# Turning the next expert's five row tiles in three groups of one, two and two

## What is computed

```python
capacity = max(1, math.ceil(N / E * CAPACITY_FACTOR))          # 4096 / 8 * 1.25 = 640 rows per expert
... # each token goes to its two best experts, as far as these have room
h = gelu(einsum('ecd,edh->ech', buf, w1) + b1[:, None, :])     # 640 x 256 by 256 x 1024
out = einsum('ech,ehd->ecd', h, w2) + b2[:, None, :]           # 640 x 1024 by 1024 x 256
y = einsum('ned,ne->nd', gathered, weights)                    # sum over a token's experts, by gate
x = layernorm(x + y)
```

## Time and profile before

| | |
|---|---|
| median of 3 runs | 917.41 us (916.76 to 917.43) |
| profiled execution, its own time | 918.83 us |
| its span in the trace | 917.0 us |
| mean granted TensorE clock | 0.986 of 2.4 GHz |
| TensorE busy | 878.5 us, 96% of the span |
| ScalarE busy | 736.7 us, 80% |
| VectorE busy | 635.7 us, 69% |
| GpSimd busy | 481.5 us, 53% |

### The profile page before, as it was taken

How to read it: one execution, slowest core, us unless ns; L and a number is a source line. 1 busy time by engine, 2 the same in 40 slices (tenths; PEclk the granted TensorE clock), 3 DMA queues, 4 the chain that set the end, 5 groups by cost and what they waited for, 6 DMA issues and landing times. The chain is left out here.

```text
span 917.0 us, 20105 instructions
## 1 busy us (share of the span) xinstructions
PE 878.5 (96%) x7673; PEld 498.4 (54%) x7673; DVE 635.7 (69%) x1177; ACT 736.7 (80%) x911; POOL 481.5 (53%) x408
## 2 busy tenths in 40 slices
PE   7999999999999999999999999999399999999995
PEld 5434344433344434334443433333299999999995
DVE  5788556547886645799565577527657887888786
ACT  5698978897897899889789889898355787778875
POOL 3388245245575635657563454441512556666574
PEclk9999999999999999999999999999789999999998
DMA  5644456643535345263433525612170745534411
GB/s 176 161 131 140 145 211 222 226 168 106 185 128 213 119 131 208 87 206 135 165 110 111 195 87 182 205 54 84 60 244 32 242 151 185 172 115 134 157 63 64
DMA packets 62508, 135.47 MB, mean 148 GB/s; under 512 B 10558, under 2 KB 31398, under 8 KB 62272
## 3 DMA queue, kind: packets, MB, share of 16 engines
q1 hardware_dynamic: 41648, 72.61, 24.4%
q0 software_dynamic: 20464, 61.18, 19.0%
q10 hardware_dynamic: 288, 0.27, 0.1%
HBM read 69.20 MB, written 62.35 MB: 143 GB/s over the span
## 5 line engine op out<-in xcount | busy, mean ns | idle before, releaser
L814 ACT ACTIVATE prob<-spsum 128x1024 f32<-128x1024 f32 x512 | 492.7, 1022 | 83.0 <-PE spsum L1036 79.2
L1060 PE MATMUL opsum<-prob,val 128*17 128x512 f32 x2048 | 270.1, 597 | 3.9 <-ACT prob L814 1.9
L1036 PE MATMUL spsum<-stacks 32*128 32x512 f32 x1536 | 135.5, 426 | 2.0 <-issue 1.3
L1036 PEld LDWEIGHTS spsum<-stacks 32*128 32x128 f32 x1536 | 73.5, 183 | 117.0 <-ACT prob L814 65.8
L1036 PEld LDWEIGHTS spsum<-area_q 32*128 32x128 f32 x1536 | 73.1, 183 | 112.7 <-ACT prob L814 57.1
L1036 PE MATMUL spsum<-area_q 32*128 32x512 f32 x1536 | 132.7, 425 | 1.1 <-ACT prob L814 1.1
L1452 DVE RECIPROCAL oden<-oden 128x256 f32<-128x256 f32 x62 | 108.7, 1753 | 2.1
L608 POOL TENSOR_TENSOR area_s<-emb,area_s 128x1024 fp32r<-128x1024 f32 x28 | 66.7, 2380 | 48.4 <-DVE area_s L1259 45.0
L694 POOL TENSOR_TENSOR onorm<-oraw,oden 128x512 f32<-128x512 f32 x31 | 42.1, 1358 | 93.3 <-DVE oden L1452 93.2
L1060 PEld LDWEIGHTS opsum<-prob,val 128*17 128x17 f32 x2048 | 39.4, 95 | 84.9 <-ACT prob L814 46.2
L606 POOL TENSOR_TENSOR square<-raw 128x512 bf16<-128x512 f32 x28 | 52.5, 1877 | 56.4 <-DVE raw L1232 56.3
(11 more groups left out here) (278 smaller groups left out, 1375.8 us busy)
## 6 DMA issues: line engine op xcount, KB each, us to landing
split_scratch<-area_s POOLq DMA_DIRECT2D x56, 512.0 KB
area_k<-in_w SPq DMA_DIRECT2D x16, 1024.0 KB, 6.9
area_q<-split_scratch SPq DMA_DIRECT2D x28, 512.0 KB
stacks<-split_scratch SPq DMA_DIRECT2D x24, 512.0 KB
rows<-dispatched SPq DMA_DIRECT2D x7, 662.5 KB
aT<-onorm SPq DMA_DIRECT2D x124, 32.0 KB
staged<-in_xT SPq DMA_DIRECT2D x7, 512.0 KB, 4.2
dispatched<-last_rows POOLq DMA_DIRECT2D x2, 1722.5 KB, 13.1
```

Source lines behind the costliest of these rows:

```text
L814: act.activation(prob[u % NPB][:], spsum[u % NSB][:].rearrange("p a n -> p (a n)"), ACT.Exp, scale=HD ** -0.5).then_inc(s_exp, 1)
L1036: ins = pe.matmul(spsum[u % NSB][:, j % 2, :], kst[par][rows, a, P * kt:P * (kt + 1)], qst[par][rows, b, cols], start=i == 0, stop=i == 2 ...
L1060: ins = pe.matmul(opsum[32 * j:32 * j + HD + 1, :], val[b % 2][:, kt, h0 + j, :], prob[(2 * s + j // 2) % NPB][:, HALF * (j % 2):HALF * (j ...
```

## The change

For every expert but the first, the five tiles are turned in three groups: tile 0, tiles 1 and 2, tiles 3 and 4. TensorE makes the four transposes of a pair one after the other into the 512 columns of one bank; ScalarE casts the pair with one operation of 512 columns, VectorE subtracts with one of 512 columns. TensorE turns tiles 1 and 2 where it turned tile 1, tiles 3 and 4 where it turned tile 2. ScalarE and VectorE handle tiles 1 and 2 where they handled tile 1, tiles 3 and 4 where they handled tile 3. The banks `tp` still alternate, by group now. The first product of the next expert waits for the second group, the seventh for the third.

```diff
+        TURNED = ((0, 1), (1, 3), (3, ST))
+        def turned_number(e, t):
+            return ST + len(TURNED) * (e - 1) + t if e else t
+        def turned_tiles(e, t):
+            return TURNED[t] if e else (t, t + 1)
+        def turned_in(e, t):
+            t0, t1 = turned_tiles(e, t)
+            return turned_bank(turned_number(e, t))[:, 0:DIM * (t1 - t0)].rearrange(
+                "p (t k n) -> p k t n", t=t1 - t0, k=KC)
+        def turned_out(e, t, part):
+            t0, t1 = turned_tiles(e, t)
+            return xe[e % 2][:, part, :, P * t0:P * t1].rearrange("p k (t n) -> p k t n", t=t1 - t0)
...
             def turn(e, t):
-                n = ST * e + t
+                n = turned_number(e, t)
...
-                if e and n >= 2:
-                    pe.wait_ge(s_turned, n - 1)
-                for k in range(KC):
-                    ins = pe.transpose(turned_bank(n)[:, P * k:P * (k + 1)],
-                                       rows[e % 2][:, t, P * k:P * (k + 1)], ident[:])
+                for i, tile in enumerate(range(*turned_tiles(e, t))):
+                    for k in range(KC):
+                        ins = pe.transpose(turned_bank(n)[:, DIM * i + P * k:DIM * i + P * (k + 1)],
+                                           rows[e % 2][:, tile, P * k:P * (k + 1)], ident[:])
...
-                            pe.wait_ge(s_turned, ST * e + -(-CH * (h + 1) // P))
+                            pe.wait_ge(s_turned, turned_number(e, 1 + h) + 1)
...
-                    if e + 1 < EXPERTS and t != 1:
+                    if e + 1 < EXPERTS and t in (0, 2):
                         turn(e + 1, t)
...
-                act.copy(xe[e % 2][:, 0, :, P * t:P * (t + 1)],
-                         turned_bank(n)[:, 0:DIM].rearrange("p (k n) -> p k n", k=KC)).then_inc(s_xhi, 1)
+                act.copy(turned_out(e, t, 0), turned_in(e, t)).then_inc(s_xhi, 1)
...
-                        if t:
-                            turned_high(e + 1, t)
+                        if t in (1, 3):
+                            turned_high(e + 1, (t + 1) // 2)
...
-                dve.tensor_tensor(lo, src, hi.bitcast(F32), ALU.subtract).then_inc(s_turned, 1)
+                dve.tensor_tensor(turned_out(e, t, 1), turned_in(e, t), turned_out(e, t, 0).bitcast(F32),
+                                  ALU.subtract).then_inc(s_turned, 1)
...
-                    if e + 1 < EXPERTS and t >= 2:
-                        turned(e + 1, t)
+                    if e + 1 < EXPERTS and t == 3:
+                        turned(e + 1, 2)
```

More of the change, by code:

```diff
@@ L1578, in turned_bank @@
         def turned_bank(n):
-            return (tp[0][:], tp[1][:], yp[0][:], yp[1][:], hp[1][:, 0])[n] if n < ST else tp[n % 2][:]
+            return (tp[0][:], tp[1][:], yp[0][:], yp[1][:], hp[1][:, 0])[n] if n < ST else tp[(n - ST) % 2][:]
+        TURNED = ((0, 1), (1, 3), (3, ST))
[10 more added lines that the diff above has]
+            return xe[e % 2][:, part, :, P * t0:P * t1].rearrange("p k (t n) -> p k t n", t=t1 - t0)
         def first_rows(eng, t):
@@ L1690, in turn @@
             def turn(e, t):
-                n = ST * e + t
+                n = turned_number(e, t)
                 if e:
                     pe.wait_ge(s_rows[e % 2], 16 * ((e + 1) // 2))
+                    pe.wait_ge(s_turned, n - 1)
                 else:
                     pe.wait_ge(s_first[t], 16)
-                if e and n >= 2:
-                    pe.wait_ge(s_turned, n - 1)
-                for k in range(KC):
-                    ins = pe.transpose(turned_bank(n)[:, P * k:P * (k + 1)],
-                                       rows[e % 2][:, t, P * k:P * (k + 1)], ident[:])
+                for i, tile in enumerate(range(*turned_tiles(e, t))):
+                    for k in range(KC):
+                        ins = pe.transpose(turned_bank(n)[:, DIM * i + P * k:DIM * i + P * (k + 1)],
+                                           rows[e % 2][:, tile, P * k:P * (k + 1)], ident[:])
                 ins.then_inc(s_turn, 1)
@@ L1933, in turned @@
                 dve.wait_ge(s_turn, n + 1)
-                src = turned_bank(n)[:, 0:DIM].rearrange("p (k n) -> p k n", k=KC)
-                hi, lo = (xe[e % 2][:, i, :, P * t:P * (t + 1)] for i in range(2))
                 dve.wait_ge(s_xhi, n + 1)
-                dve.tensor_tensor(lo, src, hi.bitcast(F32), ALU.subtract).then_inc(s_turned, 1)
+                dve.tensor_tensor(turned_out(e, t, 1), turned_in(e, t), turned_out(e, t, 0).bitcast(F32),
+                                  ALU.subtract).then_inc(s_turned, 1)
             def remainder(e, t):
```

## The result

The changed kernel takes 924.36 us (median of 4 runs, 922.53 to 926.9) against 917.42 us for the kernel before (4 runs, 916.76 to 918.63): ratio 1.0069, 95% interval 1.0043 to 1.0094. That is outside the predicted range of 916.4 to 918.2 us, and on the side that had a chance of 0.06.

The account below looks back on a forecast made before the run. TensorE's own work was taken as the bound from 672 to 882 us. Summed: 0 for TensorE, about -0.1 us for the small stall at tile 2, 0 for the rest; from the median 917.41 to 917.3 us, range 916.4 to 918.2.

Parts of the forecast that it names:

- TensorE: Second halves: a block of four transposes costs 0.44 us, so 14 fewer blocks save 0; clock stays 1.00.
- the bound of 0.42 us: Most TensorE could gain: 0.03 us per block, if low products' 0.94 against 0.91 us belongs to it, over 14 blocks.
- ScalarE and VectorE: Merged 512-column operations: cast 607 ns, subtraction 0.69 us; savings of 1.7 and 2.1 us over seven experts, hidden under TensorE.
- The slack of `high_part` of tile 2: TensorE's products waiting for `add_own` of tile 0: slack grows to some 0.5 us as TensorE comes 0.44 us later.
- Tile 3's `add_own`: VectorE, behind the second pair: 0.12 us later, delaying the release of GpSimd's scatter of tile 3.
- its queue frees it at 761.10 anyway: GpSimd's scatter of tile 3: `add_own` comes 0.12 us later, but GpSimd's queue sets its start, so no effect.
- The tail: Behind expert 6's last scatter: GpSimd's 1.12 us wait for TensorE swallows any small shift; the rest is untouched.
- C: Rival: split too late, TensorE waits for w1's remainder at each next expert's first product; 3.5 us, 920.9; chance 0.04.
- E: Rival: tail's gather or scatter shifts, or GpSimd's queue falls differently; up to 1 us either way, 916.4 to 918.4; chance 0.06.
- D: Rival: clock falls to 1.2 GHz behind a block of four; one tile per expert gives 21 us, 938; chance 0.01.

Follow-up runs that it names:

- mend 1: Also experiment 1: changed kernel with the last pair's VectorE subtraction moved behind `add_own` of tile 3; 912.63 us against 912.36 for the kernel before, ratio 1.0009.
- experiment 2: Kernel before plus two small unused VectorE copies (0.4 us together) before `add_own` of tile 3, experts 0 to 6; 921.13 us against 912.36, ratio 1.0102.
- experiment 5: Changed kernel run once more, unaltered; 924.69 us against 918.0 for the kernel before, ratio 1.0065.
- experiment 3: Changed kernel with SP's load of the next w2 held until the sums' scatters have landed; 911.93 us against 912.36 for the kernel before, ratio 0.9995.
- experiment 6: Kernel before plus one small VectorE copy (about 0.2 us) before `add_own` of tile 3; 921.06 us against 918.0, ratio 1.0032.

## Why the prediction was wrong

- **TensorE** was right: a block of four is 0.44 us, in the first trace of the changed kernel the clock stayed at 1.00 through the experts, and the summed steps of the kernel with mend 1 are 202.06 us from expert 0 to 7 against 202.40. The -0.34 us lies in the bound of 0.42 us that I gave.
- **ScalarE and VectorE** were right in size (577 and 687 ns), and that their busy time doesn't matter too.
- **The slack of `high_part` of tile 2** was wrong. I gave it 0.5 us, as only TensorE moved. `add_own` of tile 0 has a second releaser, the landing of the output scatter of the expert before last (`s_out`), and the trace before showed it by a wait of 0.17 us in expert 2. I took the place's own instruction and didn't follow the wait behind it into GpSimd's queue.
- **Tile 3's `add_own`** was mis-sized: I had 0.12 us later, measured is 0.30. I credited 0.15 us for tile 2's skipped subtraction. Its step in the queue is only 0.34 us, not 0.42, and `add_own` of tile 1 was 0.09 us later behind TensorE's moved products, so nothing of the credit was left when the second pair came.
- **The step that failed** is the sentence on that scatter: "its queue frees it at 761.10 anyway". The 0.42 us of idle time in that row say the opposite: between scatters that wait for nothing GpSimd idles 0.30 us, and this one came 0.79 us behind the end of `add_own` (760.31), in the changed kernel 0.78 us behind (757.42 and 758.20). It followed its release, not its queue. I let the delay end there. I didn't ask what the next instruction of GpSimd would meet 0.3 us later, and that is a VectorE operation of 2.36 us and behind it a load of 1 MB. In the kernel before the output scatter began 0.25 us before the one (762.37 and 762.62) and the sums' scatter ended 0.31 us before the other (764.70 and 765.01): two margins smaller than the shift of 0.30 us or about equal to it. What the runs showed in its place: a shift of this kind alone, 0.4 us in the kernel before, costs 8.8 us (experiment 2), and with the shift taken out of the changed kernel nothing is lost (experiment 1).
- **The tail** was wrong for the same reason: the 1.12 us of GpSimd's wait swallow a shift of 0.3, but not the end of the sums' scatter coming 1.9 us later.
- Of the rivals none had this mechanism. C had the slower sign with another place; E had GpSimd's queue falling differently, with a chance of 0.06 and at most 1 us. D had the clock falling behind a block of four, which no trace shows; where the clock did fall (experiment 5), it was behind a wait of 1.86 us, and it made that wait cost 3.7 us.

## What to carry to other kernels

An operation merged on an engine with slack still moves the release of whatever stands behind it. Follow that release through each queue that it enters until it is absorbed by a wait with a measured length; "issue" in a row of GpSimd is no such wait. Where a small scatter on which a later wait hangs ends a few tenths of a microsecond before the issue of a large load, that order is a cliff: give it a semaphore, or put the scatter first. Test by delaying alone; a delay of 0.4 us per expert told in one run what the whole change had hidden.

## What was unexpected of the hardware

- GpSimd's indirect scatters of 0.97 us take up to 2.01 us when they start under a long operation of VectorE, and end 0.84 to 0.85 us behind its end in the rows shown. This held for `tensor_tensor` of two SBUF inputs and for a copy of one.
- A scatter of 128 rows of 1 KB has landed 1.55 us behind its end when no load is in front of it (SP's load in experiment 3). The gathers that wait for it start 5.5 us behind its end when a 1 MB load is issued 1.6 us before that end. By what way the load delays the landing isn't shown.
- The cost has a threshold: 0.02 us of start time (2.48 to 2.50 us) decide over 1.0 us of scatter and 3.8 us of an expert (experiment 6).
- A wait of TensorE can cost twice its length: behind waits of 1.86, 1.97 and 2.21 us the granted clock was 0.50 for 3.4 us, and these experts were 3.7 to 4.1 us longer.
